# A fused block kernel: the scans spread evenly over its units, and three of them placed behind the next unit's first sums of squares

## What is computed

```python
x = x + 0.5 * ffn(layernorm(x), A, B, W, bias)
x = x + attn(layernorm(x), W_xproj, W_dt, b_dt, A_log, D_param)
x = x + 0.5 * ffn(layernorm(x), A, B, W, bias)

def ffn(x, A, B, W, bias):                       # A: 64 experts of rank 16
    vecs = einsum('arh,bsh->bsar', A, x)
    _, idx = top_k(norm(vecs, axis=-1), 4)
    routes = one_hot(idx, 64).sum(-2) / 4
    v = einsum('bsa,bsar->bsr', routes, vecs)
    delta = einsum('bsa,ajr,bsr->bsj', routes, B, v)
    return einsum('bsh,jh->bsj', x, W) + bias + delta

def attn(x, W_xproj, W_dt, b_dt, A_log, D):      # 16 states per channel
    delta_r, B_t, C_t = split(einsum('btd,rd->btr', x, W_xproj))
    delta = softplus(delta_r @ W_dt.T + b_dt)
    h = exp(delta * A) * h + delta * B_t * x     # along time
    return sum(h * C_t) + x * D
```

## Time and profile before

| | us |
|---|---|
| median of 3 runs | 2841.19 |
| lowest, highest | 2835.08, 2842.59 |
| the profiled execution | 2846.45 |
| its span, from first to last instruction | 2844.7 |
| PE busy | 2612.2 (92%) |
| POOL busy | 2349.2 (83%) |
| DVE busy | 2218.2 (78%) |
| ACT busy | 1499.8 (53%) |

### The profile page before, as it was taken

One profiled execution on the slowest core, in us unless ns is written; L12 is line 12 of the kernel. 1 busy time (PEld: TensorE's weight loads), 2 busy tenths in 40 slices (PEclk: granted clock), 3 DMA queues, 4 the chain that ended last, 5 costly groups with the idle time before them and its releaser, 6 DMA issues.

```text
span 2844.7 us, 39804 instructions
## 1 busy us (share of the span) xinstructions
PE 2612.2 (92%) x13597; PEld 1183.5 (42%) x13664; DVE 2218.2 (78%) x2933; ACT 1499.8 (53%) x3363; POOL 2349.2 (83%) x703
## 2 busy tenths in 40 slices
PE   4989999999999999898999989999999998888999
PEld 1444444444344444343444434444444433444444
DVE  8447878878888788787878878788788887887843
ACT  5355656565555554555555545555455454555521
POOL 2038988999999998899999989999899998988920
PEclk8999999999999999999999999999999999999999
DMA  5144444544454444544453445544454444453321
GB/s 217 55 113 131 138 126 130 158 147 129 135 143 133 145 122 140 133 135 139 135 162 114 136 134 155 152 125 126 140 157 143 135 127 125 137 138 126 99 63 52
DMA packets 303520, 373.50 MB, mean 131 GB/s; under 512 B 148435, under 2 KB 220243, under 8 KB 303318
## 3 DMA queue, kind: packets, MB, share of 16 engines
q1 hardware_dynamic: 286422, 337.40, 40.2%
q10 hardware_dynamic: 16896, 33.56, 4.0%
HBM read 234.05 MB, written 103.29 MB: 119 GB/s over the span
## 4 chain that ended last, share of the span: by engine, by line
PE 35%; DVE 33%; ACT 8%; DMA 8%; DVEq 7%; issue 5%; POOL 2%; ACTq 1%; SPq 1%; POOLq 0%
DVE mreg L1136 18%; PE pv L544 12%; PE po L544 7%; PE pv L548 6%; PE po L548 4%; ACT pA L922 3%; DMA delta_scratch<-mreg 3%; DMA mreg<-xnT_scratch 2%; PE py L710 2%; DVE pv L1097 2%; DVEq L1052 2%; PE pv L673 2%; DVE sel L1105 2%; DVE sel L1094 2%; DVEq L1102 2%
## 5 line engine op out<-in xcount | busy, mean ns | idle before, releaser
L512 POOL TENSOR_TENSOR mreg<-mreg 128x2048 f32<-128x2048 f32 x256 | 1161.6, 4538 | 70.8 <-ACT hst L908 70.6
L1136 DVE TENSOR_TENSOR_SCAN mreg<-pA,hst,mreg 128x512 f32<-128x512 f32 (+1 forms) x1024 | 1038.6, 1065 | 77.9 <-ACT hst L908 58.1
L922 ACT ACTIVATE pA<-mreg,nA 128x512 f32<-128x512 f32 (+1 forms) x1280 | 742.4, 596 | 458.6 <-DVE mreg L1136 415.9
L502 POOL TENSOR_TENSOR mreg<-mreg 128x1024 f32<-128x1024 f32 x340 | 795.8, 2365 | 223.4 <-DMA mreg<-delta_scratch 209.9
L544 PE MATMUL pv<-wA,xT 128*128 128x512 f16 x2016 | 471.9, 389 | 59.9 <-ACT xT L829 49.0
L544 PE MATMUL po<-wB,uT 128*128 128x512 f16 x2016 | 472.1, 383 | 15.6 <-DVE xin L1060 10.9
L544 PE MATMUL po<-wW,xT 128*128 128x512 f16 x2016 | 467.4, 380 | 6.5 <-issue 4.5
L496 POOL TENSOR_TENSOR mreg<-mreg 128x2048 f32<-128x2048 f32 x86 | 390.2, 4537 | 20.8 <-issue 20.8
L544 PEld LDWEIGHTS pv<-wA,xT 128*128 128x128 f16 x2016 | 196.0, 100 | 343.3 <-ACT xT L829 96.1
L1078 DVE TENSOR_REDUCE n<-sel 128x32 f32<-128x512 f32 x128 | 87.0, 680 | 306.5 <-ACT sel L837 306.4
L544 PEld LDWEIGHTS po<-wB,uT 128*128 128x128 f16 x2016 | 191.3, 98 | 293.5 <-issue 71.7
(11 more groups left out here) (132 smaller groups left out, 2376.4 us busy)
## 6 DMA issues: line engine op xcount, KB each, us to landing
mreg<-delta_scratch SPq DMA_DIRECT2D x256, 512.0 KB, 6.0
delta_scratch<-mreg ACTq DMA_DIRECT2D x128, 256.0 KB
xin<-x SPq DMA_DIRECT2D x32, 512.0 KB, 5.2
x_scratch<-xin SPq DMA_DIRECT2D x32, 512.0 KB, 3.9
xnT_scratch<-auxs SPq DMA_DIRECT2D x32, 512.0 KB, 2.9
mreg<-xnT_scratch SPq DMA_DIRECT2D x64, 256.0 KB, 7.0
yT_scratch<-mreg SPq DMA_DIRECT2D x64, 256.0 KB, 2.3
uT<-yT_scratch SPq DMA_DIRECT2D x32, 512.0 KB, 4.6
```

The lines of the kernel that those rows point to most:

```text
L502: pool.tensor_tensor(h[:, half * n:half * n + n, :], u, b.broadcast_to([P, n, c.width]), ALU.mult).then_inc(s_bm, 1)
L512: pool.tensor_tensor(h, h, by_c, ALU.mult).then_inc(s_cm, 1)
L922: last = nc.scalar.activation(dst[:, part, :], src[:, part, :], ACT.Exp, scale=nA[:, m:m + 1])
L1136: last = V.tensor_tensor_scan(h, split(pA[:, i % 2, :], c)[:, part, :], h, before, ALU.mult, ALU.add)
```

## The change

Nothing is computed otherwise. Each unit gets a first and a last block, `block0` and `block1`, so that the 1024 blocks are spread over the 57 units evenly: 18 in each (17 in units 3 and 31). A unit that had four groups begins with no block or one ahead of its slots, one that had five with two or three. `block_at` spreads a unit's blocks over the twenty points: 9 lie before point 10, 13 before point 14, 14 before point 15. `sum_up` of tile t now stands before block 16t+25 wherever that falls, and not before block 16t+24 at the start of a slot. On DVE the last piece is `scans(17, 20)`, three scans, behind `sums(b, 0)`; ahead of that stands `scans(15, 17)`, one scan. The order of PE, POOL and SP is as before.

```diff
+    for a in us[SCAN0:SCAN1]:
+        a.block0 = (a.u - SCAN0) * 4 * NGRP // (SCAN1 - SCAN0)
+        a.block1 = (a.u + 1 - SCAN0) * 4 * NGRP // (SCAN1 - SCAN0)
+    us[SCAN1].block0, us[SCAN1].block1 = 4 * NGRP, 4 * NSL
...
-        def blocks_in(a):
-
-            groups = [g for g in a.slots if g < NGRP]
-            return (4 * groups[0], 4 * len(groups)) if groups else (0, 0)
+        def block_at(a, twentieths):
+
+            return a.block0 + (twentieths * (a.block1 - a.block0) + 10) // 20
...
                 def decays(lo, hi):
 
-                    for i in range(lo, hi):
-                        if count and i < count + 2:
-                            decay(first + i)
+                    if SCAN0 <= a.u < SCAN1:
+                        for i in range(block_at(a, lo - 2), block_at(a, hi - 2)):
+                            decay(i + 2)
...
-            def sum_up(a, n):
-
-                S = slot_of(a, n)
-                if S is None or S < 6 or (S - 6) % 4:
-                    return
-                t = (S - 6) // 4
+            def sum_up(t):
+
                 dve.wait_ge(s_e, 4 * t + 4)
...
                 def scans(lo, hi):
-                    for i in range(lo, hi):
-                        if i % 4 == 0:
-                            sum_up(a, i // 4)
-                        if i < count:
-                            scan(first + i)
+                    for i in range(block_at(a, lo), block_at(a, hi)):
+                        if i % 16 == 9 and i >= 24:
+                            sum_up(i // 16 - 1)
+                        if i < 4 * NGRP:
+                            scan(i)
...
-                scans(15, 18)
+                scans(15, 17)
                 result(a, 1)
                 delta(a, 2)
                 if a.kind == 1:
                     dve.drain()
                     dve.wait_ge(s_xn2, a.w)
                     stats("ln2", xin[:, a.p, :], s_mv2)
-                scans(18, 20)
                 if b:
                     sums(b, 0)
+                scans(17, 20)
```

More of the change, by code:

```diff
@@ L26, in __init__ @@
         self.slots = []
+        self.block0, self.block1 = 0, 0
         self.zs = {}
@@ L926, in unit @@
                 late = l if l and l.kind == 1 else None
-                first, count = blocks_in(a)
                 def decays(lo, hi):
-                    for i in range(lo, hi):
-                        if count and i < count + 2:
-                            decay(first + i)
+                    if SCAN0 <= a.u < SCAN1:
+                        for i in range(block_at(a, lo - 2), block_at(a, hi - 2)):
+                            decay(i + 2)
                 if a.u == SCAN0:
```

## The result

| | us | ratio to before, with its 95% interval |
|---|---|---|
| before, median of 4 runs | 2841.89 | |
| after, median of 4 runs (2875.72 to 2880.35) | 2877.71 | 1.0131 [1.0113, 1.0150] |
| after, profiled execution (its span) | 2877.66 (2875.9) | |

One execution of the kernel before, taken with the first experiments, ran at a granted clock of 0.61 and took 4079 us; it enters no ratio.

What follows compares the result with a forecast made beforehand. No engine is full; a loop through PE, ACT and DVE leaves PE some 3 us idle per unit. Terms 21 + 0 - 10 - 4 + 8 - 3 = +12 us gave 2853 us, range 2815 to 2882.

Steps and rivals of the forecast that it cites:

- term e: Adding up y one block later: in units from 32 on PE's states product waits for it; +8 us, bounds 0 and +15.
- Term a: 15 four-group kind 1 units: second squares 2.96 us later behind decays, less saved scan and cushions; 1.4 each, +21 us.
- the cushion: Kind 1, four groups: slack at PE's delta product (1.54 us) and DVE's decay wait (0.77 us), expected to absorb delay.
- Term b: 14 five-group kind 1 units: second squares 1.3 us later on average, less 1.19; taken as 0, bounds -5 and +9.
- Term c: 28 kind 2 units, no refinement: second squares 0.54 us later, less 1.19; -0.35 each, -10 us, bounds -18 and 0.
- Term d: DVE's wait for x in units 32, 40 and 56: delta's copy goes out 1.3 us sooner; -4 us, bounds 0 and -10.
- Term f: POOL's 70.6 us wait for ACT's saved last columns eases in five-group units; -3 us, bounds 0 and -20.
- each unit gives the loop 1.19 us at that place: Between choice and next statistics stand 9 scans instead of 10, so each unit saves one scan of 1.19 us.
- The signs I had named: Trace checks: unit 34's second squares 3 us later; kind 2 statistics 0.5 to 0.7 sooner; units 30 to 47 grow, 48 to 59 shrink.
- Full delay: Rival: late squares pass through all kind 1 units, DVE reaching statistics no earlier; 2876 to 2896 us, chance 0.17.
- Even feeding: Rival: POOL's rhythm sets the pace and half its 70.6 us come back; 2809, between 2795 and 2830, chance 0.23.
- Cushions that swallow all: Rival: idle time of DVE and PE absorbs the delays, so no change; about 2841 us, chance 0.18.

Runs made afterwards that it cites:

- the first experiments: The first follow-up runs, each half of the change by itself: the even spread 2805.89 us, the last scans behind the sums on the kernel before 2876.47 us.
- Even alone: The kernel after, evenly spread, but with all scans of a unit back ahead of the next first sums: 2805.89 us, 0.9878.
- even with ten: Even spreading with all scans ahead of the sums, but ten scans ahead of the next statistics in place of nine, decays moved to match: 2840.2 us, 1.0001.
- squares first: On ACT the second squares moved ahead of the last two decays: on the kernel after 2814.91 us; with even spreading and scans ahead of the sums 2789.13 us.
- place alone: The kernel before, uneven as it was, with the last scans, from 17 on, moved behind the first sums of squares: 2876.47 us, 1.0133.

## Why the prediction was right in direction and short in size

The forecast, slower by a little with ACT's queue as the cause, stands; its +12 should have been +36. My delays before any gain come to 15 x 2.96 + 14 x 1.3 + 28 x 0.54 = 77 us. Measured by the start of the second sums they are 3.0, 0.9, 0.7 and 0.7 us in the four classes, 76 us in all. That side was right in total, though not in each class. The gains and term e were not. A class of the table holds term e too, so I set beside each class what is left of it in the run with y added up one block earlier, where PE waits for `sum_up` no longer than before (6.1 us): +34, -4, +5 and -16 us against before. These are differences of single profiles and good to a few us.

- **Term a** (kind 1, four groups; +21). The mechanism is the one in the rows. Over the 15 units the second sums come 3.0 us later (9.61 to 12.63 behind the low part), where I had 2.96, and in unit 35 PE's delta product waits 1.10 us where I had 1.42. But the class lost 30 us, 2.0 per unit, and 34 without term e. The saved scan came back in full: the statistics end 1.86 us later, which is 3.0 less 1.15. What failed is the cushion: I let DVE's 0.77 and PE's slack take off another 0.37, and they took nothing. That is beyond my 1.0 to 1.8 per unit, inside my outer bound.
- **Term b** (kind 1, five groups; 0, bounds -5 and +9). The class lost 11. The second sums come 0.85 us later (11.69 to 12.54), less than my 1.3, yet from there to the statistics it takes 0.14 us more than before in place of 1.19 less. With y added up earlier the class is 4 us shorter than before. So the 0 was sound for what it named, and most of the loss is term e's.
- **Term c** (kind 2; -10). It came to -9: 1 and -10, and to -11 without term e. In unit 35 the second squares start 0.43 us later behind the low part, and I had 0.54. The near hit is partly luck: the saved scan gave 1.3 and 1.6 us up to the statistics, more than its length, and against that the ends of units 14 and 22 lost 3.4 and 3.2 us, which no step of mine had: there the blocks run ahead of the groups' slots and reach a tile before its delta has landed. POOL, ACT and DVE in unit 15 of the kernel after:

```profile
766.56 4.68 POOL L506 TENSOR_TENSOR mreg<-mreg 128x1024 f32<-128x1024 f32 x2 [6.55 <-DMA mreg<-delta_scratch]
...
768.94 0.69 ACT L926 ACTIVATE pA<-mreg,nA 128x512 f32<-128x512 f32 x1 [4.00 <-DMA mreg<-delta_scratch]
...
771.28 2.46 DVE L1139 TENSOR_TENSOR_SCAN mreg<-pA,hst,mreg 128x512 f32<-128x512 f32 x2 [2.49 <-POOL mreg L506]
```

- **Term d** (load of x; -4). Zero. In unit 32 DVE's wait fell from 3.49 to 1.82 us, as I said. But units 56 and 48 wait longer, and the four waits add up to 8.6 us where there were four of 9.4.

```profile
1516.77 0.69 DVE L1063 TENSOR_TENSOR xin<-pt,xin 128x512 f32<-128x512 f32 x1 [1.82 <-DMA xin<-x_scratch]
```

- **Term e** (`sum_up`; +8, bounds 0 and +15). It cost 18. I named the mechanism and the place, and counted at most 1 us in eleven units from 32 on. There PE waited 13 times for it, 0.6 to 3.2 us each (1.89 in unit 34) and 27 us in all. In the units before 32, of which I had none, it waited 14 us, where it was 6.5 before.
- **Term f** (POOL's saved columns; -3). The wait fell by 54 us and the time did not: it went to deltas and to PE, as I had written, so it is worth nothing that these runs show.

**The step that failed.** The direction and the mechanism held; three sizes did not. Term e is 10 us short, because I counted one short wait where PE waits 2 us each time, and in units that I had left out. Term a is 9 us short as the class stands and 13 without term e, because I let cushions shorten a delay that they did not shorten. And terms d and f took off 7 us that never came. Against that stand 4 us of term b and 1 of term c: 10 + 13 + 7 - 4 - 1 = 25, where 24 are missing. What I credited everywhere, "each unit gives the loop 1.19 us at that place", is 68 us. From the second sums to the statistics after took 56 us less than before, 1.0 per unit, but 12 us were lost again from there to the next low part, 8 of them at units 14 and 22. So, in the profiles, 76 of delay less 56 plus 12 make the 32 us of the 57 units. Even alone is the same case with losses already taken off: in its profile the stretch up to the statistics gives 52 us and the next one costs 12, and PE waits 23.7 us for `sum_up`.

**The signs I had named.** In unit 34 the second squares start 2.8 us later behind the first sums, right behind two decays. In kind 2 the second sums come 0.7 us later and the next statistics 0.65 and 0.93 us sooner. The units 30 to 47 grew, by 0.58 us each. Those of kind 2 alone, 48 to 59, shrank by 1.6 us in all twelve, too little to tell from nothing. POOL's waits for saved columns fell by 54 us, but its waits taken together grew.

**The rivals.** Full delay gave 2876 to 2896, and the time lies in it. Its condition was that DVE reaches the statistics no earlier than now. In unit 35 they end at 1655.92, which is 34.85 us behind the low part, against 32.46 before, and over the classes of kind 1 they end 1.9 and 1.0 us later, in kind 2 0.65 and 0.93 us sooner. So it holds in kind 1, and describes it better than my forecast did. Yet its upper end, +55 in kind 1, isn't what happened: kind 1 lost 41, and kind 2 gave back 9. Even feeding finds no support as a mechanism (even with ten), and that its number for a faster kernel, 2809, is close to that of even alone doesn't support it. Cushions that swallow all is out.

**What stays open.** The tiles that had not landed in units 15 and 23 are only seen in the trace; a version that shifts the blocks was not tried. That both gates must lose a scan rests on pairs of runs that differ in the spread too; a kernel with nine and fourteen scans on the uneven plan was not run. How the 36 us divide between terms a, e and the lost tiles rests on one profile of each kernel. And the price of DVE's wait for softplus (19.0 us in total, 3.1 before) was not measured by itself.

## What to carry to other kernels

When work moves between two steps of one engine, look at where its partner stands on the other engine that takes its orders in turn: here the scans' new place cost 72 us, and reordering only ACT's decays, squares and normalisation won 87 (squares first alone also gave 17 us with the scans in their old place). A step saved in a loop counts only as far as every gate behind it also opens sooner; look at the waits of the engine that is fed, gate by gate, before crediting its length. A step moved from ahead of a gate to behind it is not saved; it is saved when it goes where the engine stands idle. And two edits that are each small in one kind of unit can meet in another: place alone left the four-group units untouched, and spreading brought them the delay.
